# A bidirectional selective-scan kernel: 15 of 64 tiles get u*B with time on the partitions

## What is computed

```python
xn = layernorm(x); xp = xn @ proj.T + pb; z = silu(xp)
for each direction (forward, and backward over reversed time):
    xs = softplus(xp @ conv.T + cb)
    delta_r, B, C = split(xs @ dbc.T, [32, 48])        # B, C: 16 states each
    delta = softplus(delta_r @ dtp.T + dtb)            # per channel
    dA  = exp(delta[..., None] * A)                    # (time, 256, 16)
    dBu = delta[..., None] * B[:, None, :] * xs[..., None]
    h_t = dA_t * h_(t-1) + dBu_t                       # the scan
    y_t = sum over n of h_t[:, n] * C_t[n]  + xs * D
out = x + z * (y_forward + y_backward)
```

## Time and profile before

| | |
|---|---|
| median of 3 runs | 20609.74 us (20606.74 to 20610.97) |
| the profiled execution's own time | 20590.7 us |
| its span, first to last instruction | 20588.9 us |
| DVE busy | 19678.2 us (96%) |
| POOL busy | 19541.0 us (95%) |
| PE busy | 14397.9 us (70%) |
| ACT busy | 11798.2 us (57%) |
| moved by DMA | 4494 MB, 218 GB/s |

### The profile page before, as it was taken

One profiled execution on the slowest core, in us unless ns is written; L12 is line 12 of the kernel. 1 busy time (PEld: TensorE's weight loads), 2 busy tenths in 40 slices (PEclk: granted clock), 3 DMA queues, 4 the chain that ended last, 5 costly groups with the idle time before them and its releaser, 6 DMA issues.

```text
span 20588.9 us, 254528 instructions
## 1 busy us (share of the span) xinstructions
PE 14397.9 (70%) x76320; PEld 9682.2 (47%) x76320; DVE 19678.2 (96%) x11520; ACT 11798.2 (57%) x12601; POOL 19541.0 (95%) x8658
## 2 busy tenths in 40 slices
PE   6676766767676776767767767676776767677676
PEld 4444444444444444444444444444444444444444
DVE  7999999999999999999999999999999999999999
ACT  5555555655556555555655555555565555556554
POOL 7999999999999999999999999999999999999999
PEclk8999999999999999999999999999999999999998
DMA  6667676767667666666767667676676666767666
GB/s 203 216 219 219 220 221 217 220 217 224 216 218 224 215 221 218 218 219 218 224 216 221 218 216 221 216 222 219 218 223 216 219 221 218 221 219 223 215 221 199
DMA packets 1214177, 4494.01 MB, mean 218 GB/s; under 512 B 161408, under 2 KB 172160, under 8 KB 1163392
## 3 DMA queue, kind: packets, MB, share of 16 engines
q1 hardware_dynamic: 1078912, 3934.73, 55.4%
q0 software_dynamic: 82944, 503.35, 12.6%
q10 hardware_dynamic: 50688, 36.88, 0.7%
HBM read 3945.94 MB, written 134.22 MB: 198 GB/s over the span
## 4 chain that ended last, share of the span: by engine, by line
issue 40%; DVE 30%; PE 17%; ACT 5%; POOL 4%; DVEq 1%; DMA 1%; ACTq 1%; POOLq 0%
DVE ring L926 20%; DVE bv L910 9%; PE y L761 6%; PE bank L788 5%; PE bv L751 4%; POOL ring L392 2%; ACT dA L571 2%; DMA c<-c_rows 1%; PE bank L782 1%; ACT tmp L579 1%; ACT bv L571 1%; DVE w L941 1%; PE bank L841 1%; ACT pre L579 1%; ACT pre L583 1%
## 5 line engine op out<-in xcount | busy, mean ns | idle before, releaser
L392 POOL TENSOR_TENSOR ring<-ring,c 128x1024 f32<-128x1024 f32 x6144 | 14689.5, 2521 | 950.3 <-DVE ring L926 613.0
L926 DVE TENSOR_TENSOR_SCAN ring<-dA,bv 128x1024 f32<-128x1024 f32 x4992 | 11199.2, 2273 | 209.4 <-ACT dA L571 62.4
L571 ACT ACTIVATE dA<-delta,a_step 128x1024 f32<-128x1024 f32 x4992 | 5606.4, 1145 | 3232.9 <-DVE ring L926 2914.7
L751 PE MATMUL bv<-parts,select 128*128 128x512 bf16 x9984 | 3307.0, 416 | 5533.2 <-DVE ring L926 5522.0
L761 PE MATMUL y<-ident,ring 128*128 128x128 f32 x49152 | 6923.1, 292 | 171.9 <-POOL ring L392 170.5
L761 PEld LDWEIGHTS y<-ident,ring 128*128 128x128 f32 x49152 | 6343.1, 153 | 1377.1 <-POOL ring L392 320.4
L910 DVE TENSOR_TENSOR bv<-u,bv 128x1024 f32<-128x1024 f32 x4992 | 5944.6, 1214 | 525.9 <-PE bv L751 504.2
L751 PEld LDWEIGHTS bv<-parts,select 128*128 128x128 bf16 x9984 | 706.1, 101 | 7496.1 <-DVE ring L926 7087.7
L571 ACT ACTIVATE bv<-delta,a_step 128x1024 f32<-128x1024 f32 x1152 | 1287.3, 1117 | 3381.3 <-DVE ring L926 3381.1
L402 POOL TENSOR_TENSOR v<-u,v 128x1024 f32<-128x1024 f32 x1152 | 2855.8, 2479 | 0.0
L926 DVE TENSOR_TENSOR_SCAN ring<-bv,v 128x1024 f32<-128x1024 f32 x1152 | 2608.6, 2264 | 0.9
(11 more groups left out here) (71 smaller groups left out, 10215.2 us busy)
## 6 DMA issues: line engine op xcount, KB each, us to landing
c<-c_rows SPq DMA_DIRECT2D x6144, 512.0 KB, 4.8
v<-c_rows SPq DMA_DIRECT2D x1152, 512.0 KB, 5.3
w<-pre POOLq DMA_DIRECT2D x96, 1024.0 KB, 12.3
xf<-tmp POOLq DMA_DIRECT2D x96, 1024.0 KB, 10.9
delta<-pre POOLq DMA_DIRECT2D x96, 1024.0 KB, 8.0
delta<-tmp POOLq DMA_DIRECT2D x96, 1024.0 KB, 10.1
pre<-out_dram SPq DMA_DIRECT2D x88, 1024.0 KB, 7.1
out_dram<-z POOLq DMA_DIRECT2D x96, 512.0 KB, 10.2
```

The source lines that it names most:

```text
L392: nc.gpsimd.tensor_tensor(ring[k % NR][:], ring[k % NR][:], c_sb[k % NC][:], ALU.mult).then_inc(p_ready, 1)
L571: nc.scalar.activation(to[:], delta_of(d, s)[:, c, :], ACT.Exp, scale=a_step[s][:, c, n:n + 1]).then_inc(da_ready, 1)
L751: mm = pe.matmul(bv[k % 2][:, half(h)], select[:, n:n + 1].to_broadcast([P, P]), parts_of(d, s)[:, half(h)], start=True, stop=True)
L926: nc.vector.tensor_tensor_scan(h, a, b, 0.0, ALU.mult, ALU.add).then_inc(h_ready, 1)
```

## The change

A third kind of tile is brought in beside the plain and the shared ones. In 15 **turned** tiles (7, 11, 15, ... 63) u x B is computed with time on the partitions: B of one state is then one number per partition, which ScalarE can apply as a scale.

- Once for each of the four blocks of 16 tiles, TensorE turns u in eight 128x128 transposes into bank (`turn_u`, slots 1, 13, 28, 43) and ScalarE copies it out to u_t (`u_out`, 128x1024).
- Twice a step, TensorE turns dbc (which holds B and C) and ScalarE copies the B of the four states out to b_t (128x32).
- For a turned tile ScalarE does eight ACTIVATEs of 128x128, u_t x b_t, into the one buffer v_t (new `times_b` of ScalarE, right after the exp of the tile two before). TensorE turns them back into bv (`turn_v`) in the place of `rep_b`. VectorE only scans.
- The shared tiles are 8 instead of 12 (6, 14, ... 62), with one buffer v instead of two; plain tiles are 41 instead of 52.
- The three dA and eight ring buffers (11) become ten common ones: the exp writes where the scan then writes over it, in place. The exp of tile k therefore waits for the sum of tile k-9 (or k-10).
- Sums run with LAG 5, HELD 7, where it was 4 and 6; SEED, B_AHEAD, V_AHEAD and the tables of the preparation are laid anew. mean_w is one column, repeated by its access pattern.

```diff
-    NDA, NR, NC, NV = 3, 8, 4, 2
-    SEED = 8
-    SHARED = (7, 11, 15, 21, 25, 29, 35, 39, 45, 49, 57, 61)
-    B_AHEAD, V_AHEAD = 7, 6
-    LAG, HELD = 4, 6
+    NB_TILE, NC, NV = 10, 4, 1
+    SEED = 10
+    SHARED = (6, 14, 22, 30, 38, 46, 54, 62)
+    B_AHEAD, V_AHEAD = 6, 5
+    TURN_FROM, TURN_EVERY = 3, 4
+    TURNED = tuple(k for k in range(TILES) if k % TURN_EVERY == TURN_FROM and k >= TURN_EVERY)
+    TURNS = NS // TURN_EVERY
+    VT_AHEAD = 2
+    LAG, HELD = 5, 7
...
-    CONV_AT = ((19, 21, 23, 25), (25, 25, 29, 31))
+    CONV_AT = ((14, 15, 17, 18), (19, 20, 24, 25))
...
+    U_TURN_AT, U_OUT_AT = (1, 13, 28, 43), (1, 13, 29, 44)
...
+        tile = [sb(f"tile{i}", [P, T]) for i in range(NB_TILE)]
...
+        u_t = sb("u_t", [P, T // P, P])
+        v_t = sb("v_t", [P, T // P, P])
+        b_t0 = sb("b_t0", [P, T // P, TURNS])
+        b_t1 = [sb(f"b_t1_{s}", [P, T // P, TURNS]) for s in range(2)]
...
+        CYCLES = (9, 9, 9, 9, 9, 9, 10)
+        assert sum(CYCLES) == TILES and max(CYCLES) == NB_TILE
+        PLACE = [i for n in CYCLES for i in range(n)]
+        def tile_of(k):
+            return tile[PLACE[k]]
+        def gap(k):
+            return next(g for g in range(1, TILES + 1) if PLACE[(k - g) % TILES] == PLACE[k])
...
-                    act.wait_ge(h_ready, tiles(it, k + 1 - da_gap(k)))
-                    to = dA[da_of(k)]
+                    act.wait_ge(summed, tiles(it, k + 1 - gap(k)))
+                    to = tile_of(k)
                 nc.scalar.activation(to[:], delta_of(d, s)[:, c, :], ACT.Exp,
                                      scale=a_step[s][:, c, n:n + 1]).then_inc(da_ready, 1)
+            def u_out(it, b):
+                act.wait_ge(u_turned, it * 4 + (b + 1))
+                act.wait_ge(v_t_ready, CHUNKS * turns(it, b * NS))
+                nc.scalar.copy(u_t[:].rearrange("p q c -> p (q c)"), banks[:]).then_inc(u_t_ready, 1)
+            def times_b(it, k, s):
+                d, n = (k // NS) % DIRS, k % NS
+                act.wait_ge(u_t_ready, it * 4 + (k // NS + 1))
+                act.wait_ge(b_t_ready, it * 2 + 2)
+                act.wait_ge(v_back, turns(it, k))
+                for q in range(CHUNKS):
+                    nc.scalar.activation(v_t[:, q, :], u_t[:, q, :], ACT.Copy,
+                                         scale=b_t(d, s)[:, q, n // TURN_EVERY:n // TURN_EVERY + 1]).then_inc(v_t_ready, 1)
...
+                    if k == B_OUT_AT[j]:
+                        act.wait_ge(b_turned, n * 2 + (j + 1))
+                        nc.scalar.copy(b_t(d, s)[:], banks[:].rearrange("p (q n) -> p q n", n=P)[:, :, TURN_FROM:NS:TURN_EVERY]
+                                       ).then_inc(b_t_ready, 1)
...
+                    if k + VT_AHEAD in TURNED:
+                        times_b(it, k + VT_AHEAD, s)
+                    if k - AHEAD in U_OUT_AT:
+                        u_out(it, U_OUT_AT.index(k - AHEAD))
...
+            def turn_u(it, s, b, more):
+                c, d = b // DIRS, b % DIRS
+                n = it + 1
+                pe.wait_ge(u_ready, it * 2 + 2)
+                if b > 0:
+                    pe.wait_ge(u_t_ready, it * 4 + b)
+                if b == 0 and more:
+                    pe.wait_ge(centred, n * 2 + 2)
+                if b == 1 and more:
+                    pe.wait_ge(xp_ready, n * FILLS + FILLS)
+                if b == 1 and not early(it, 1):
+                    pe.wait_ge(gated, it * DT)
+                if b == 2 and more:
+                    pe.wait_ge(conv_out, n * (2 * FILLS) + 2 * FILLS)
+                if b == 3:
+                    pe.wait_ge(gated, it * DT + 1)
+                for q in range(CHUNKS):
+                    mm = pe.transpose(banks[:, chunk(q)], u_of(d, s)[:, c, chunk(q)], ident[:])
+                mm.then_inc(u_turned, 1)
+            def turn_v(it, k):
+                pe.wait_ge(h_ready, tiles(it, k - 1))
+                pe.wait_ge(v_t_ready, CHUNKS * turns(it, k + 1))
+                for q in range(CHUNKS):
+                    mm = pe.transpose(bv[k % 2][:, chunk(q)], v_t[:, q, :], ident[:])
+                mm.then_inc(v_back, 1)
...
+                    if k == B_TURN_AT[j]:
+                        pe.wait_ge(dbc_out, n * 4 + (2 * j + 2))
+                        for q in range(CHUNKS):
+                            mm = pe.transpose(banks[:, chunk(q)], dbc[:, chunk(q)], ident[:])
+                        mm.then_inc(b_turned, 1)
...
+                    elif k + 2 in TURNED:
+                        turn_v(it, k + 2)
...
-                dve.wait_ge(summed, tiles(it, k + 1 - NR))
+                h = tile_of(k)[:]
                 if k in SHARED:
+                    dve.wait_ge(summed, tiles(it, k + 1 - gap(k)))
                     dve.wait_ge(vp_ready, others(it, k + 1))
                     a, b = bv[k % 2][:], v_sb[SHARED.index(k) % NV][:]
                 else:
-                    dve.wait_ge(v_ready, own(it, k + 1))
-                    a, b = dA[da_of(k)][:], bv[k % 2][:]
-                h = ring[k % NR][:]
+                    if k in TURNED:
+                        dve.wait_ge(v_back, turns(it, k + 1))
+                    else:
+                        dve.wait_ge(v_ready, own(it, k + 1))
+                    a, b = h, bv[k % 2][:]
```

More of the change, by code:

```diff
@@ L122, in xs_of, with b_t @@
             return w[s] if d else xf[s]
+        def b_t(d, s):
+            return b_t1[s] if d else b_t0
         scratch = (pre, tmp)
-        dA = [sb(f"dA{i}", [P, T]) for i in range(NDA)]
-        ring = [sb(f"ring{i}", [P, T]) for i in range(NR)]
+        tile = [sb(f"tile{i}", [P, T]) for i in range(NB_TILE)]
         c_sb = [sb(f"c{i}", [P, T]) for i in range(NC)]
@@ L146, in conv_seq_kernel @@
         diag_d = [sb(f"diag_d{s}", [P, DT, P]) for s in range(2)]
-        mean_w = sb("mean_w", [P, P])
+        mean_w = sb("mean_w", [P, 1])
         select = sb("select", [P, NS], BF16)
@@ L202, in conv_seq_kernel @@
         y_back = sem("y_back")
+        u_turned = sem("u_turned")
+        u_t_ready = sem("u_t_ready")
+        b_turned = sem("b_turned")
+        b_t_ready = sem("b_t_ready")
+        v_t_ready = sem("v_t_ready")
+        v_back = sem("v_back")
         da_ready = sem("da_ready")
@@ L220, in own, with turns @@
         def own(it, k):
-            return it * (TILES - len(SHARED)) + (k - sum(t < k for t in SHARED))
+            return it * (TILES - len(SHARED) - len(TURNED)) + (k - sum(t < k for t in SHARED + TURNED))
         def others(it, k):
             return it * len(SHARED) + sum(t < k for t in SHARED)
-        DA = {}
-        for k in range(TILES):
-            if k not in SHARED:
-                DA[k] = len(DA) % NDA
-        if DA[max(DA)] == DA[min(DA)]:
-            DA[max(DA)] = (DA[max(DA)] + 1) % NDA
-        def da_of(k):
-            return DA[k]
-        def da_gap(k):
-            return next(g for g in range(1, TILES + 1) if DA.get((k - g) % TILES) == DA[k])
+        def turns(it, k):
+            return it * len(TURNED) + sum(t < k for t in TURNED)
+        CYCLES = (9, 9, 9, 9, 9, 9, 10)
[5 more added lines that the diff above has]
+            return next(g for g in range(1, TILES + 1) if PLACE[(k - g) % TILES] == PLACE[k])
         CHAINS = 4
@@ L436, in prepare @@
                             pool.wait_ge(vp_ready, others(n - 1, TILES - NS))
+                            pool.wait_ge(u_turned, (n - 1) * 4 + 3)
                         nc.gpsimd.tensor_tensor(u_of(d, s)[:], delta_of(d, s)[:], xs_of(d, s)[:],
@@ L760, in add_up @@
                 for q in range(CHUNKS):
-                    mm = pe.matmul(y[:, chunk(q)], ring[k % NR][:, chunk(q)], ident[:], is_transpose=True,
+                    mm = pe.matmul(y[:, chunk(q)], tile_of(k)[:, chunk(q)], ident[:], is_transpose=True,
                                    start=(k % HALF_TILES == 0 and q % (CHUNKS // NH) == 0),
@@ L799, in prepare @@
                             pe.wait_ge(gated, (n - 2) * DT + 1)
-                        over_channels(bank[h], lambda c: mean_w[:], pre, h).then_inc(mean_ready, 1)
+                        over_channels(bank[h], lambda c: mean_w[:].to_broadcast([P, P]), pre, h).then_inc(mean_ready, 1)
                     if k == VAR_AT[h]:
+                        if not early(n, 1):
+                            pe.wait_ge(u_t_ready, (n - 1) * 4 + 1)
                         pe.wait_ge(squared, n * 2 + (h + 1))
                         pe.wait_ge(centred, n * 2 + (h + 1))
-                        over_channels(bank[h], lambda c: mean_w[:], pre, h).then_inc(var_ready, 1)
+                        over_channels(bank[h], lambda c: mean_w[:].to_broadcast([P, P]), pre, h).then_inc(var_ready, 1)
                 for i, (e, h) in enumerate(layers_steps):
@@ L821, in prepare @@
                                 pe.wait_ge(xp_ready, n * FILLS + FILLS)
+                                if not (j or early(n, 1)):
+                                    pe.wait_ge(u_t_ready, (n - 1) * 4 + 2)
```

(10 more changed lines are left out.)

37 lines of the change are left out of this document (21 added, 16 removed).

## The result

The changed kernel takes 21504.83 us (median of 4 runs, 21464.0 to 21513.85), the kernel before 20608.24 in the same comparison: ratio 1.0435, 95% interval 1.0423 to 1.0448. I had forecast 19,585 and a range up to 20,400. The profiled execution's span is 21,502.9 us.

A forecast was written before the change was run, and what follows sets the result against it. VectorE and GpSimd were both taken as full, GpSimd the longer afterwards: 194.2 + 3.7 + 2.6 + 2.0 = 202.5 us a step; 95 steps, 19,238, plus ends of 328 led to 19,585 us (5.0% less), range 19,100 to 20,400.

The forecast's parts named there:

- The work of each engine: Work per step after the change: VectorE 192.1 us, GpSimd 194.2 (the floor), ScalarE 163.6, TensorE 163.0.
- The waits after: Waits added to GpSimd's work per step: 3.7 us for C, 2.6 for scans, 2.0 for exps behind held sums.
- (d): VectorE's 4.5 us of waits for bv; turn_v's 0.87 us against rep_b's 0.45 taken to cancel with VectorE's 2 us slack.
- All else stays, only at other slots: GpSimd's other work (64 products, norm, u, parts, DMAs) stays, only at other slots; just four v go, 9.3 us.
- (c): ScalarE's exp of k waits for the sum of k-9; late only behind the held sums, 2 us a step.
- Late scales: Rival, slower: the chain exp, scales, turn_v, scan holds TensorE up; slower from 1.4 us per turned tile; 20,970 us, chance 7%.
- One buffer v: Rival: C loads behind the eight v loads come late, 5.2 to 10.4 us a step; 20,130 to 20,560 us, chance 12%.
- The clock: Rival: TensorE rests at the lower clock, transposes not counting as activity; 74 us a step more, 22,860 us, chance 3%.
- What would show it: Wrong if scans wait over 10 us for ScalarE, GpSimd over 8 for C, clock well under 0.92, or 2.32/2.19 us change.

The follow-up runs named there:

- b_ten: The kernel before with only the buffers changed: ten common ones, scans in place, LAG 5, HELD 7; 20593.86 us, ratio 1.0001.
- g_odd: f_tabs with two v buffers instead of one and the shared tiles moved to 9, 13, 21, ... 61; 19972.06 us, ratio 0.9697.
- a_free: The changed kernel without ScalarE's eight scales, turned tiles getting bv from rep_b's two matmuls; u and dbc still turned; 21548.09 us, ratio 1.0467.
- f_base: The changed kernel without any turning (u, dbc, v_t), a turned tile being rep_b and a scan; 21168.55 us, ratio 1.0281.
- b_tabs: The kernel before with the changed kernel's tables of the preparation alone (VAR_AT to GATE_AT); 21319.38 us, ratio 1.0350.
- f_tabs: f_base with the kernel before's tables for the preparation, copies, gatings and skips; 20568.58 us, ratio 0.9989.
- f_both: f_base with both the tables and the buffers of the kernel before; 20736.19 us, ratio 1.0068.
- b_half: The kernel before with the preparation's matrix products over one half of the channels instead of two; 20788.17 us, ratio 1.0093.
- a_rest: The changed kernel with GpSimd's two rest subtractions moved from slots 38 and 49 to 41 and 52; 21482.03 us, ratio 1.0435.
- f kernels: Four kernels without any turning, with changed or earlier tables and buffers; 20568.58 (f_tabs) to 21233.46 us.

## Why the prediction was wrong, by its own steps

- **The work of each engine** was right: 193.6, 194.7, 161.6 and 163.9 us a step measured, against 191 to 192, 194.2, 163.6 and 163.0. A scan in place costs what the other did (2.29 us for one; b_ten 1.0001). A pair of bare scans that waited for nothing took 4.38, but only half of them did so.
- **The waits after** are the step that failed. I put 8.3 us a step on GpSimd, 3.7 for C, 2.6 for scans and 2 for the held sums, taken from the waits of the kernel before. Measured: 26.8, of it 16.3 for scans, 8.7 at rest and 1.8 for C. With 194.7 of work that is 221.5, of a step of 222.0 in these seven.
- Inside it, **(d), "I let these cancel"**, is where the 16.3 come from: VectorE's waits for bv were 4.5 us a step before, priced as unchanged, and are (95.0 + 39.5) / 7 = 19.2. I used TensorE's 70% share as cover. In each slot it does a `rep_b` that waits for a scan, then sums, then preparation, and nothing can be done ahead. By the prediction's own prices a slot with one product over channels holds 0.45 + 0.87 + 5.32 / 3 = 3.1 us, of the 3.3 that a plain tile takes and against 2.2 in a bare pair (an estimate). The change left eight pairs 4.38 us, put eight transposes in 21 places a step and set the preparation closer. `g_odd` (355 us), `a_free` against `f_base` (380, for the turns of u and dbc) and `b_tabs` (728) show each of these in the time, each in another kernel.
- **"All else stays, only at other slots"**: the tables were priced at nothing. Alone they cost 728 us in the kernel before, with a lower clock, and 600 between `f_base` and `f_tabs`. 225 of the 728 went with two GpSimd instructions put ahead of the matmuls and the DMA they wait for (rest in slot 49, dtp's last matmul in slot 51: it could be read from the tables).
- **(c), exps behind sums**: no loss of its own; b_ten 1.0001, f_tabs better than f_both.
- **Late scales**, the rival for slower at 7%: the sign came true, the mechanism as written not. Without scales and turns the changed kernel is no faster. In `g_odd`'s kernel the chain costs 10 us a step, 0.67 us for each turned tile, less than the 1.4 at which I had it decide, and, as its waits read, more by filling ScalarE than by late scales. Scans waited (39.5 + 22.9) / 7 = 8.9 us a step for turned tiles and exps, just under the 10 set as its sign.
- **One buffer v** (12%): real, 241 us in f_tabs (with the clock up from 0.883 to 0.909); in the changed kernel C waits are small because GpSimd stands elsewhere.
- **The clock** (3%): did not drop in the changed kernel (0.910 against 0.918), though 11 `rep_b` went and 21 groups of transposes came. The Trainium skill ("TensorE: Matmul & The Clock Gate", Part 4: PE-mode transpose) says that transposes don't count as activity. That is not borne out here: sixteen in a row, behind matmuls, ran at a granted 1.00 (9137.61, 1.91 us). My own stretch for it was read too strongly: 9115.20 to 9119.60 holds 16 transposes, 16 matmul records with diag_d and two `rep_b`, so half of it is matmuls. The clock fell elsewhere: with less for TensorE to do (b_half 0.873, a_free 0.885) and with the same matmuls in other slots (b_tabs 0.867).
- **What would show it**: none of the signs of being wrong came true, though the step was 20 us over. C took 1.8 us a step (sign: over 8), scans 8.9 for ScalarE (over 10), the clock was 0.910, a product took 2.32 us (6.96 for three) and a scan 2.19. I had set no sign on GpSimd's wait for scans or VectorE's for `rep_b`, and the loss stood there.

What stays open: how the 897 us divide. The parts measured alone (tables 728, u and dbc 380, chain 949, pattern 355, v 241, less the 11 us a step of VectorE's work) add up to more than the whole; `a_rest` shows one of them hidden under another wait, for the rest that is argued. Open too is how much of the b_tabs and f kernels' times is the lower clock.

## What to carry to other kernels

When two engines are full and a third is in order between them, its share of busy time is no cover. Count for each stretch between two of its waits what stands in it, and hold that against the time that the faster engines will now leave. A loss that an edit removes without effect may only be covered: take the largest away first, or test it in a kernel that has room, before calling it free. Places in a hand-written order are part of a change's price, and each moved instruction that waits has to be checked against where its producer now stands.

## What the runs showed of the hardware

With 20 of a step's products left out (40 records, some 17 us of TensorE's time) the kernel before got slower by 0.9%, and TensorE's mean granted clock went from 0.918 to 0.873; that the clock is the reason is likely but not isolated. The same matmuls in other slots had 0.867 (`b_tabs`). Mean granted clocks of the profiled runs were between 0.867 and 0.929 (`g_odd`). Each fp32 128x512 matmul of the code left two records in the trace, 0.44 us apart at full clock (12 in 5.32 us), each transpose one. A scan on VectorE that writes over its own first operand in SBUF takes 2.28 us in the median, as one to another buffer does (L1021 after and L926 before).
